# Statistics of the first norm for batches 1 to 3 moved from VectorE to ScalarE, in two accumulating passes

## The reference

```python
m = jnp.mean(x, axis=-1, keepdims=True)
v = jnp.var(x, axis=-1, keepdims=True)
xn = (x - m) / jnp.sqrt(v + 1e-5)
q = xn @ Wq.T                      # 16 heads of 16
# each row attends to 4 rows of a 128-row context, chosen by seg_id
x = x + tanh(g_xattn) * (softmax(q . k_sel / 4) @ v_sel) @ Wo.T
x = x + tanh(g_ffn) * ffn(layernorm(x))
```

## Time and profile before

| | us |
|---|---|
| median of 3 runs | 355.43 |
| lowest and highest | 355.17, 357.68 |
| the profiled execution | 353.4 |
| its span, first to last instruction | 351.6 |
| VectorE busy | 316.8 (90% of the span) |
| TensorE busy | 289.5 (82%) |
| ScalarE busy | 207.7 (59%) |
| GpSimd busy | 171.8 (49%) |

### The profile page before, as it was taken

The page is one execution under the profiler, slowest core; times in us unless marked ns, Lnnn a source line. Parts: engine busy times, 40 slices in busy tenths (PEclk is TensorE's granted clock), DMA queues, the critical chain, the costliest instruction groups (busy, mean ns, idle before and its releaser), DMA issues.

```text
span 351.6 us, 5786 instructions
## 1 busy us (share of the span) xinstructions
PE 289.5 (82%) x1807; PEld 210.5 (60%) x1807; DVE 316.8 (90%) x614; ACT 207.7 (59%) x323; POOL 171.8 (49%) x160
## 2 busy tenths in 40 slices
PE   3873779767679999999999955699799949999994
PEld 3442557555557777777777734344344418888883
DVE  0988599999998999999999999779999879999993
ACT  2132341251605666555556635899699969999991
POOL 1100638849497989889989882012243500110000
PEclk9998588885969999999999999699999998999999
DMA  7993000000000000000000000011112100435545
GB/s 259 282 389 111 0 0 0 2 1 0 2 2 0 0 2 0 3 0 2 1 2 1 3 0 0 0 62 60 60 61 102 77 1 2 62 60 76 98 64 119
DMA packets 6979, 17.26 MB, mean 49 GB/s; under 512 B 1318, under 2 KB 3822, under 8 KB 6446
## 3 DMA queue, kind: packets, MB, share of 16 engines
q1 hardware_dynamic: 4447, 12.31, 9.8%
q0 software_dynamic: 1008, 3.67, 6.8%
q10 hardware_dynamic: 1503, 1.02, 1.2%
HBM read 9.13 MB, written 7.86 MB: 48 GB/s over the span
## 4 chain that ended last, share of the span: by engine, by line
DVE 51%; PE 35%; issue 4%; ACT 4%; DMA 2%; POOL 2%; DVEq 0%; ACTq 0%; POOLq 0%
PE bank L786 16%; PE bank L756 12%; DVE prod L863 10%; DVE s L869 8%; DVE s L875 4%; PE bank L593 4%; DVE bn L820 3%; DVE xres L917 2%; DMA wq_ld<-in_L_xattn_Wq_dram 2%; PE bank L613 2%; DVE hmax L1117 2%; DVE onehot L969 2%; DVE xmax L923 2%; DVE s L884 2%; DVE bn L830 2%
## 5 line engine op out<-in xcount | busy, mean ns | idle before, releaser
L593 PE MATMUL bank<-kvtab,onehot 80*128 80x256 f16 x512 | 73.2, 291 | 26.3 <-DVE prod L863 17.1
L593 PEld LDWEIGHTS bank<-kvtab,onehot 80*128 80x128 bf16 x512 | 49.8, 103 | 46.1 <-DVE prod L863 22.4
L298 POOL TENSOR_TENSOR vsel<-vsel,pr 128x1024 f32<-128x1024 f32 x31 | 59.9, 1932 | 25.9 <-ACT vsel L348 20.3
L485 ACT ACTIVATE hidden<-bank,bin__58,zscale 128x512 f32 x64 | 49.6, 777 | 7.4 <-PE bank L756 2.2
L756 PE MATMUL bank<-xhi,win 128*128 128x512 f16 x128 | 49.3, 385 | 1.9 <-DVE xlo L1112 1.9
L756 PE MATMUL bank<-xlo,win 128*128 128x512 f16 x128 | 49.1, 384 | 0.0
L1177 DVE SCALAR_TENSOR_TENSOR hlo<-hq,rel_wout,hhi 128x512 f16<-128x512 int16 x64 | 46.0, 752 | 0.0
L863 DVE TENSOR_TENSOR prod<-bank,q 128x1024 f32<-128x1024 f32 x32 | 39.0, 1218 | 5.4 <-PE bank L593 5.3
L348 ACT ACTIVATE xT<-bank 128x512 f32<-128x512 f32 x16 | 9.5, 597 | 55.5 <-PE bank L644 55.5
L348 ACT ACTIVATE vsel<-bank 128x1024 f32<-128x1024 f32 x31 | 31.6, 1018 | 17.1 <-PE bank L593 17.1
L301 POOL TENSOR_TENSOR vsel<-vsel 128x512 f32<-128x512 f32 x31 | 40.4, 1302 | 2.4
(11 more groups left out here) (133 smaller groups left out, 479.8 us busy)
## 6 DMA issues: line engine op xcount, KB each, us to landing
xres<-in_x_dram SPq DMA_DIRECT2D x4, 1024.0 KB, 17.7
out_dram<-xres SPq DMA_DIRECT2D x7, 512.0 KB, 2.6
out_dram<-y POOLq DMA_DIRECT2D x7, 512.0 KB, 5.3
win_ld<-in_L_ffn_W_in_dram SPq DMA_DIRECT2D x1, 1024.0 KB, 12.4
wout_ld<-in_L_ffn_W_out_dram SPq DMA_DIRECT2D x1, 1024.0 KB, 23.1
seg_i<-in_itok_BxS_dram SPq DMA_DIRECT2D x3, 320.0 KB, 13.9
wkv_ld<-in_L_xattn_Wkv_dram SPq DMA_DIRECT2D x1, 512.0 KB, 4.9
seg_i<-in_itok_BxS_dram ACTq DMA_DIRECT2D x1, 320.0 KB, 9.2
```

The source lines that it names most:

```text
L298: pool.tensor_tensor(v3, v3, pr[k][:, t].rearrange("p o h -> p (o h)").unsqueeze(2).broadcast_to([P, KW * H, HD]), ALU.mult).then_inc(s_pv, 1)
L485: act.activation(hidden[:, g, f, :], bank, ACT.Gelu, bias=bin_[:, f:f + 1], scale=zscale[:, f:f + 1]).then_inc(s_h, 1)
L593: mm = pe.matmul(dst[:, off * D:(off + 1) * D], onehot[:, off, bass.ds(tile * P, P)], kvtab[:, b, part, col:col + D], start=(part == 0), s ...
```

## The change

VectorE's three calls of `stats1` in steps 4, 5 and 6 go. ScalarE gets a `stats1(b, half)` that handles four tiles (half a batch): four Copy activations over 256 columns whose output is never read and whose accumulated row sums are kept, one small activation that turns the sums into minus the means, and four Square activations with that as the bias, whose accumulated sums are kept. It stands at the head of ScalarE's steps 2 to 7, ahead of `exp(i-2)`: batch 1 in steps 2 and 3, batch 2 in steps 4 and 5, batch 3 in steps 6 and 7. Between the three groups ScalarE waits on its own semaphores. GpSimd divides the sum of squares by 256 and adds epsilon in one instruction in place of the addition, and `inv_std1` for batches 1 to 3 moves to the head of its steps 4, 6 and 8. Batch 0 is as it was.

```diff
--- before.py
+++ after.py
@@ -125,6 +125,8 @@
         smax, ssum, srec = pair("smax", [P, 2, H]), pair("ssum", [P, 2, H]), pair("srec", [P, 2, H])
         bn1 = a_r.put("bn1", [P, TB, 6], F32)
         mv1, ve1, rstd1 = a_r.put("mv1", [P, NT, 2], F32), a_r.put("ve1", [P, NT], F32), a_r.put("rstd1", [P, NT], F32)
+        sum1, nmean1, ssq1 = a_r.put("sum1", [P, NT], F32), a_r.put("nmean1", [P, NT], F32), a_r.put("ssq1", [P, NT], F32)
+        unread = [a_r.put(f"unread{i}", [P, TB // 2, D], BF16) for i in range(2)]
         bn2 = pair("bn2_", [P, 2, 6])
         mv, ve, rstd, nbias = pair("mv", [P, 2, 2]), pair("ve", [P, 2]), pair("rstd", [P, 2]), pair("nbias", [P, 2])
         wq_mean = a_r.put("wq_mean", [P, C], F32)
@@ -184,6 +186,7 @@
         s_tanh = sem("tanh_ready")
         s_vc = sem("vector_setup_chain")
         s_bn1, s_mv1, s_ve1, s_rstd1 = sem("stats1_parts"), sem("mean_var1_ready"), sem("var1_eps_ready"), sem("rstd1_ready")
+        s_sum1, s_nmean1, s_ssq1 = sem("x_sums"), sem("x_minus_means"), sem("x_square_sums")
         s_bn2 = sem("stats2_parts")
         s_mv, s_ve, s_rstd, s_nb = sem("mean_var_ready"), sem("var_eps_ready"), sem("rstd_ready"), sem("norm_bias_ready")
         s_wqc = sem("wq_centred")
@@ -274,8 +277,12 @@
             def inv_std1(b):
 
                 at = slice(b * TB, (b + 1) * TB)
-                pool.wait_ge(s_mv1, b + 1)
-                pool.tensor_tensor(ve1[:, at], mv1[:, at, 1], consts[:, 0:TB], ALU.add).then_inc(s_ve1, 1)
+                if b == 0:
+                    pool.wait_ge(s_mv1, 1)
+                    pool.tensor_tensor(ve1[:, at], mv1[:, at, 1], consts[:, 0:TB], ALU.add).then_inc(s_ve1, 1)
+                else:
+                    pool.wait_ge(s_ssq1, 2 * b)
+                    pool.tensor_scalar(ve1[:, at], ssq1[:, at], 1.0 / D, LN_EPS, ALU.mult, ALU.add).then_inc(s_ve1, 1)
                 pool.wait_ge(s_ve1, b + 1)
                 pool.tensor_tensor(rstd1[:, at], ve1[:, at], consts[:, TB:2 * TB], ALU.pow).then_inc(s_rstd1, 1)
 
@@ -315,8 +322,8 @@
             pool.wait_ge(s_const, 3)
             inv_std1(0)
             for i in range(NP + 4):
-                if 4 <= i <= NB + 2:
-                    inv_std1(i - 3)
+                if i in (4, 6, 8):
+                    inv_std1(i // 2 - 1)
                 step(i, i % 2)
 
             pool.wait_ge(s_bias, 1)
@@ -423,6 +430,24 @@
                     ins = act.activation(q[k][:, t, :], ps_q[:, t * D:(t + 1) * D], ACT.Copy,
                                          scale=rstd1[:, 2 * u + t:2 * u + t + 1])
                 ins.then_inc(s_q, 1)
+
+            def stats1(b, half):
+
+                n = 2 * (b - 1) + half
+                act.wait_ge(s_x[b], 16)
+                if n:
+                    act.wait_ge(s_ssq1, n)
+                at = slice(b * TB + half * (TB // 2), b * TB + (half + 1) * (TB // 2))
+                for t in range(at.start, at.stop):
+                    ins = act.activation(unread[0][:, t % (TB // 2), :], xres[:, t, :], ACT.Copy, accum_out=sum1[:, t:t + 1])
+                ins.then_inc(s_sum1, 1)
+                act.wait_ge(s_sum1, n + 1)
+                act.activation(nmean1[:, at], sum1[:, at], ACT.Copy, scale=-1.0 / D).then_inc(s_nmean1, 1)
+                act.wait_ge(s_nmean1, n + 1)
+                for t in range(at.start, at.stop):
+                    ins = act.activation(unread[1][:, t % (TB // 2), :], xres[:, t, :], ACT.Square, bias=nmean1[:, t:t + 1],
+                                         accum_out=ssq1[:, t:t + 1])
+                ins.then_inc(s_ssq1, 1)
 
             def keep_win8(hf):
                 act.wait_ge(s_w8p, hf + 1)
@@ -462,6 +487,8 @@
             kv_high(2)
             kv_high(3)
             for i in range(2, NP + 2):
+                if 2 <= i < 2 * NB:
+                    stats1(i // 2, i % 2)
                 step(i, i % 2)
             evac_oT(NP - 1, 1)
             evac_xn2T(NP - 3, 1)
@@ -1047,8 +1074,6 @@
             dve.wait_ge(s_tanh, 1)
             step(3, 1)
             for i in range(4, NP + 1):
-                if i <= NB + 2:
-                    stats1(i - 3)
                 step(i, i % 2)
                 if i <= NB + 1:
                     clamp_seg(i - 2)
```

## The result

The changed kernel takes 364.95 us (median of 4 runs, 361.73 to 366.46) against 355.36 us: a ratio of 1.0243, 95% interval 1.0159 to 1.0326. Measured once more beside later experiments it took 364.08 us (362.05 to 365.71), ratio 1.0264 (1.0207 to 1.0322). So it is slower, by 9 to 10 us. The profiled execution took 366.46 us with a span of 364.6 us, 13.0 us more than the span of before; it was the slowest of its four runs.

What follows compares the result with a forecast made beforehand. VectorE was taken to bound the attention part. The profiled 353.4 us plus 10.5 for the delayed sums and 3.5 for TensorE's clock gave 367.4 us, so 369 us for the median; range 359 to 377 us.

Steps and rivals of the forecast that it cites:

- Bound and place: Attention part, about 20 to 215 us: VectorE bounds it; its sum L889 would wait for ScalarE's exponential, giving back 9.9 us.
- The wait's total: VectorE's wait at L889 for the exponential, steps 3 to 8: about 23 us in all, where one of 1.46 stood.
- S: Time of ScalarE's half batch of statistics ahead of the exponential: 5.0 us, bounds 3.1 and 6.4.
- Step 2 hidden: Step 2: sum and first product delayed 1.75 us, hidden by VectorE's 3.39 us wait for TensorE's second gather; cost 0.
- The rule 5 S - 14.5: Delay of VectorE's sums over steps 3 to 7, S minus each step's room: +10.5 us; step 5's gain stops at 3.3.
- the room of step 4: Step 4, from the exponential's end to the sum's start: 1.63 us, called wide because VectorE has first-norm statistics there.
- The clock, 3.5 us: TensorE's stretches leading to steps 4, 5 and 8 turn slow: 0.5 + 0.5 + 2.5 = 3.5 us, bounds 0 and 8.1.
- more 5s and 6s from 60 to 130 us: Sign in the changed profile: more digits 5 and 6 in TensorE's clock line between 60 and 130 us.
- GpSimd at about 0: GpSimd's moved inv_std1 goes into idle time and leaves the second norm's path: about 0, 0 to -0.7 us.
- C: Rival: VectorE's relief wins in steps 5 and 6, S below 2.9 us; 353 us at S = 2.4; chance 0.04.
- D: Rival: Square outside the active table set, two loads of 1.28 us per S, S = 7.6; 383 us; chance 0.03.
- A: Rival: cheap accumulation on ScalarE, S = 3.1 to 3.6, 2 us for the clock; 360 us; chance 0.11.

Runs made afterwards that it cites:

- experiment 1: Changed kernel with ScalarE's half batch moved from the head of the step to ahead of the xT evacuation: 348.12 us, ratio 0.9785; again 347.78 us, ratio 0.9807.
- experiment 5: Changed kernel with no first-norm statistics for batches 1 to 3 on any engine, GpSimd using those of batch 0: 348.99 us, ratio 0.9822.
- experiment 3: Changed kernel with VectorE's statistics of batches 1 to 3 put back as well, computed and not used: 365.29 us, ratio 1.0267.
- experiment 4: Changed kernel without the Copy pass and the small activation, Square pass alone, variance taken about zero: 351.50 us, ratio 0.9899.
- Experiment 6: Changed kernel with 18 useless identity transposes by TensorE in steps 3 to 8, ahead of the second v gather: 358.82 us, ratio 1.0118.

## Why the prediction was right, and where it was wrong

- **Bound and place: right.** VectorE bounded the attention part, its relief was real (experiments 1 and 5: 7 and 6 us in the end) and the wait of L889, now L916, for the exponential took it back. The relief was worth nothing in the changed kernel (experiment 3). The sums were to come 3.0, 6.3, 5.6, 5.5 and 10.5 us later in steps 3 to 7 and came 3.2, 5.7, 5.2, 4.6 and 7.9 later.
- **The wait's total: partly luck.** It is 22.8 us where I said about 23 (my own terms add up to 23.9), and from step 3 on 2.9, 5.7, 2.6, 3.3, 5.4 and 2.3 us where I said 3.0, 6.7, 2.6, 3.2, 6.4 and 2. With S at 3.94 my rule gives only 1.9, 1.5 and 2.2 us for steps 3, 5 and 6; the late queries of step 2 and the slower stretches filled up what S lacked. In the second profile the total is 19.0 us, with 0.2 in step 6, where the stretch ahead took 6.82 us.
- **Step 2 hidden: right.** The sum is 1.0 us later there, the second product 0.25 us, which is the shift that was there already.
- **S = 5.0: too dear, it is 3.94 us.** The failed term is "for the accumulated sum I add one smallest activation, 0.20 us". The reading is 0.20 us long, but the next activation starts 0.09 us behind its start. Eight times 0.11 us are most of the 1.06 us, and 1.06 five times over is 5.3 us of the total. The small activation in the middle, at 0.20 us, and the Square with its bias, 0.09 us dearer than the Copy, were right.
- **The rule 5 S - 14.5: right in kind.** With S = 3.94 it gives 5.2 us, and both profiles of the changed kernel have that much and the change of the stretches. With its floors and S = 1.60 it forecast 350 us for experiment 4, and 351.5 came. One word of the reading was off: the room of step 4, 1.63 us, is not wide; VectorE's statistics there already had most of their time from the wait that would else have stood.
- **The clock, 3.5 us: about the right size, in the wrong places.** By the medians 9.6 us were lost (9.2 the second time) and S explains 5.2, so 4.4 (3.9) are left for all the rest. I named steps 4, 5 and 8. In the profiled execution the stretches that lead to them (those that begin in steps 3, 4 and 7) lost 0.2, 1.3 and 2.6 us, but the queries of step 2 lost 0.9 us, and 2.6 us went behind step 17, which I had not in the sum at all; in the second profile the stretches lost 0.7 us in all and 4.1 went behind step 17. Experiment 6 shows that TensorE kept busy gives 5.3 us back; how the loss is shared out stays open. The sign "more 5s and 6s from 60 to 130 us" came in part: there are more 6s and 7s and no 5, and from 45 to 125 us the granted clock fell from 0.84 to 0.76 (0.80 in the second profile).
- **The sum.** Against the median the forecast was 13.6 us more and 9.6 were measured: an S priced 5.3 us too high, and some 1 us too little for the rest. That the profiled execution came at 366.5 us where I said 367.4 is luck: it was 1.5 us above its median, while the one of before was 2.0 below.
- **GpSimd at about 0: right for this kernel only.** VectorE's wait of 2.29 us in step 8 hides the inversion moved there. Where that wait is gone (experiments 5 and 6) the step takes about 1.2 to 1.4 us longer, with the waits for POOL rstd in it.
- **Rivals.** C (relief wins) needed S below 2.9 us; experiment 4, with 1.60, shows that side. D (table loads) did not come: the trace of the changed kernel has the same two table loads as the one of before, 1.283 us each, one ahead of the attention part and one in the feed-forward part. A (cheap accumulation) had S at 3.1 to 3.6, nearer to the measured 3.94 than my 4.5 to 5.5, and put 2 us on the clock where about 4 came. The measured 365 us lie between A's 360 and my 369.

## What to carry to other kernels

Idle time of an engine is not free room; where a new instruction stands in the engine's order decides. Look for the wait that the engine's own order ends next: here work placed where ScalarE next waits for TensorE's xT costs next to nothing, and the same work placed right behind the queries costs its full length wherever no room is left, and both places are in one step. Before moving work off the bounding engine, subtract, step by step, the end of what the engine waits for from the start of its own instruction: that room, not the busy share, is what the helper may take. And before pricing a wait on TensorE, price what runs behind it at the lower clock too.

## What the runs showed of the hardware

- Reading ScalarE's accumulator is an instruction of its own in these traces: 0.19 to 0.20 us long, 48 of them in this kernel. The next activation starts 0.09 us behind its start, so that the pitch of an activation of 256 columns with its sum is 0.40 us (Copy) or 0.49 us (Square with a bias from SBUF).
- The same waits of TensorE were followed by different granted clocks, so the length of a wait alone does not tell the clock behind it. In the drain of the attention part TensorE's waits are the same in both kernels (2.29 us for the last attention output), yet the output projection behind it ran in 1.99 us before the change and in 3.21 us after, at a granted clock of 0.98 and 0.70. Both rows, first of the kernel before, then of the changed one, with windows that begin within or right behind them (busy us of each engine, then the clock, DMA share, GB/s):

```profile
212.66 1.99 PE L613 MATMUL bank<-woT,oT 128*128 128x256 f32 x8 [0.69 <-ACT oT L348]
...
213.00:221.00 8.00, 4.87 (x36) 3.81 (x34) 7.65 (x22) 5.84 (x11) 1.79 (x4) 0.98 0.00 0
```

```profile
222.98 3.21 PE L640 MATMUL bank<-woT,oT 128*128 128x256 f32 x8 [0.69 <-ACT oT L355]
...
223.40:232.50 9.10, 6.39 (x33) 5.08 (x32) 7.75 (x21) 5.17 (x11) 1.76 (x4) 0.70 0.00 1
```

The second profile of the changed kernel, first the same projection behind the same waits, then the one of step 5, which took 3.62 us in the first profile (the row at 89.06 above):

```profile
218.16 3.78 PE L640 MATMUL bank<-woT,oT 128*128 128x256 f32 x8 [0.69 <-ACT oT L355]
...
86.75 1.89 PE L640 MATMUL bank<-woT,oT 128*128 128x256 f32 x8
```

What decides between the two levels in such a case, no run here shows.

- From the start of the sum in step 17 to the start of the last maximum over xn2 (`qx<-xmax`) it took 15.3 us before, 16.6 in the changed kernel, 17.2 in its second profile and in the first of experiment 1, 15.4 in experiment 6. Behind that maximum the rest of the span was up to 3.3 us longer than before in these profiles. So versions of this kernel can differ by 1 to 2 us in a part that nobody touched, and by up to some 3 us more behind it; experiment 1 is 8.3 us ahead when the attention part ends and 3.1 us at the end of the same profile (7 us by the medians). Read differences of 1 to 2 us between versions of this kernel, and single profiles above all, with that in mind.
